# A graph network kernel: three edges of one destination per lane, packed across node tiles

## The reference

```python
# layer 0: for each type r, the mean of x[src] over a node's edges of that type, times weight[r]
out = x @ root + bias
for r in range(8):
    mask = (edge_type == r)
    sums = segment_sum(x[src] * mask[:, None], dst)
    cnt = segment_sum(mask, dst)
    out = out + (sums / maximum(cnt, 1.0)[:, None]) @ weight[r]
z = concatenate([out, x]) @ w_gate + b_gate
x = layernorm(x + tanh(out) * z + x * (1.0 - z))
# layer 1: a graph convolution with self loops and symmetric norm
h = x @ W
out = segment_sum(h[src] * (dinv[src] * dinv[dst])[:, None], dst) + b
x = layernorm(x + relu(out))
```

## Time and profile before

| | us |
|---|---|
| time, median of 3 runs | 1619.83 (1618.04 to 1620.3) |
| the profiled execution's own time | 1620.98 |
| its span in the trace | 1619.2 |
| TensorE busy | 1595.0 (99%) |
| VectorE busy | 1138.9 (70%) |
| GpSimd busy | 800.8 (49%) |
| ScalarE busy | 576.2 (36%) |

### The profile page before, as it was taken

One profiled execution on the slowest core, in us unless ns is written; L12 is line 12 of the kernel. 1 busy time (PEld: TensorE's weight loads), 2 busy tenths in 40 slices (PEclk: granted clock), 3 DMA queues, 4 the chain that ended last, 5 costly groups with the idle time before them and its releaser, 6 DMA issues.

```text
span 1619.2 us, 23695 instructions
## 1 busy us (share of the span) xinstructions
PE 1595.0 (99%) x7947; PEld 1308.0 (81%) x7947; DVE 1138.9 (70%) x1908; ACT 576.2 (36%) x963; POOL 800.8 (49%) x809
## 2 busy tenths in 40 slices
PE   8999999999999999999999999999999998999997
PEld 6888888888877777788888888888888887887886
DVE  4856655655557666748878875688778878888486
ACT  4211111111133333425655553455555653122000
POOL 1000777777766666527777772677676600000000
PEclk9999999999999999999999999999999999999999
DMA  6322444445322121267877774777778886656743
GB/s 228 109 88 79 125 125 130 113 106 138 85 77 79 66 72 64 68 221 231 250 223 222 243 234 145 227 245 222 236 217 276 296 277 208 232 211 221 281 142 117
DMA packets 122123, 280.34 MB, mean 173 GB/s; under 512 B 23142, under 2 KB 24406, under 8 KB 121872
## 3 DMA queue, kind: packets, MB, share of 16 engines
q0 software_dynamic: 38256, 104.17, 22.5%
q1 hardware_dynamic: 46912, 98.19, 18.8%
q10 hardware_dynamic: 36832, 76.44, 12.6%
HBM read 209.97 MB, written 83.10 MB: 181 GB/s over the span
## 4 chain that ended last, share of the span: by engine, by line
PE 94%; DVE 3%; DMA 1%; issue 1%; ACT 1%; POOL 0%; SPq 0%; ACTq 0%; DVEq 0%; POOLq 0%
PE PG L777 67%; PE PG L966 6%; PE PG L1032 5%; PE PM L789 3%; PE PM L800 3%; PE PM L801 3%; PE PG L873 2%; PE PG L939 2%; PE PM L835 1%; DMA y<-STAGE 1%; PE PM L948 1%; PE PM L818 1%; DMA WRAW<-in_L_gnn_weight_dram 0%; PE PM L759 0%; DVE STATS L1682 0%
## 5 line engine op out<-in xcount | busy, mean ns | idle before, releaser
L777 PE MATMUL PG<-WHI,XHI 128*128 128x512 f32 x1600 | 631.5, 395 | 2.9 <-DVE WLO L1298 2.9
L777 PE MATMUL PG<-WHI,XLO 128*128 128x512 f32 x1600 | 623.6, 390 | 0.0
L777 PE MATMUL PG<-WLO,XHI 128*128 128x512 f32 x1600 | 623.0, 389 | 0.0
L777 PEld LDWEIGHTS PG<-WHI,XHI 128*128 128x128 f32 x1600 | 300.7, 188 | 65.7 <-issue 2.9
L777 PEld LDWEIGHTS PG<-WHI,XLO 128*128 128x128 f32 x1600 | 300.6, 188 | 63.6
L777 PEld LDWEIGHTS PG<-WLO,XHI 128*128 128x128 f32 x1600 | 300.8, 188 | 60.1
L1082 ACT ACTIVATE STAGE<-PG 128x512 f32<-128x512 f32 x200 | 119.2, 596 | 460.7 <-PE PG L777 460.7
L1298 DVE TENSOR_TENSOR WLO<-WRAW,WHI 128x512 fp32r<-128x512 f32 x176 | 122.2, 696 | 226.0 <-ACT WHI L1075 225.9
L710 POOL DMA_INDIRECT WORK<-y,REC x184 | 201.6, 1096 | 93.1 <-issue 46.8
L657 POOL DMA_INDIRECT records<-RREC,IDX x160 | 210.1, 1313 | 61.0 <-issue 43.7
L710 POOL DMA_INDIRECT RAW<-y,REC x184 | 202.3, 1099 | 72.0 <-issue 46.3
(11 more groups left out here) (262 smaller groups left out, 2232.5 us busy)
## 6 DMA issues: line engine op xcount, KB each, us to landing
y<-STAGE ACTq DMA_DIRECT2D x220, 256.0 KB
WRAW<-in_L_gnn_weight_dram SPq DMA_DIRECT2D x128, 256.0 KB, 3.1
EDGE_ROWS<-edge_rows POOLq DMA_DIRECT2D x10, 1000.0 KB, 6.4
WRAW<-in_L_gnn_w_gate_dram SPq DMA_DIRECT2D x32, 256.0 KB, 4.1
WORK<-y SPq DMA_DIRECT2D x15, 512.0 KB, 4.9
WORK<-x SPq DMA_DIRECT2D x10, 512.0 KB, 4.7
WORK<-in_x_dram SPq DMA_DIRECT2D x9, 512.0 KB, 3.6
XROWS<-in_x_dram SPq DMA_DIRECT2D x9, 512.0 KB
```

What stands on the lines that cost most here:

```text
L777: last = pe.matmul(PG[:, bank, :], lhs[:, k, t * P:(t + 1) * P], rhs[:, j % 2, k, :], start=(k == 0 and n == 0), stop=(k == KT - 1 and n = ...
```

## The change

Three edges of one destination share a lane (PER = 3), and lanes are packed without a break between node tiles. A node takes a third of its edges' number, rounded up, and at least one lane, so there are 62 triples of edge tiles (NTRI) instead of 92 pairs: 186 edge tiles instead of 184.

A triple's 128 lanes can now reach from one node tile into the next. `windows` finds the node at which each triple starts (with one more matmul, `count_windows`), the number of its node tile and of the next, and two masks over the 128 rows. The one-hot puts a destination at its row modulo 128, and `msg_add` adds the bank of PM twice: to the first node tile's sums under one mask, to the next one's under the other; it loads two numbers for that.

The counts are kept with the ten source tiles of a node side by side, so one addition of 1280 cells at a computed place still does for a triple; the final stage reads them with a stride of ten elements.

Counting takes 62 steps with three tiles each (six matmuls) and two sets of one-hots in flight. In the messages VectorE adds the second and the third row, the third waiting for the second; the one-hot moves to ScalarE (Square, then Relu). The ring still has eight rows, in another order of places. Steps: run 0 in 229 to 316, run 1 in 325 to 414, the first transpose of u before step 419.

Halved scales for even source tiles (DINV_SRC) make up for counts kept doubled. The diff, cut to its core:

```diff
-NPAIR = (E // 2 + N // 2 + NT * (P - 1)) // P
-ETILES = 2 * NPAIR
+PER = 3
+NTRI = ((E + PER * N) // PER + P - 1) // P
+ETILES = PER * NTRI
...
-HIGH_CELL = 1 << 16
+HIGH_CELL = 1 << 15
+ROUND = float(3 << 22)
 SPLIT = 1024
 EXACT = 256
-AHEAD = 2
-HOTS = 8
+HOTS = 2 * PER
 EARLY = 5
 SLOTS = 4
+RAWS = 8
...
-RUN0_FROM, RUN0_TO = 229, 315
-RUN1_FROM, RUN1_TO = 324, 413
-TURN0_STEP = 417
+RUN0_FROM, RUN0_TO = 229, 317
+RUN1_FROM, RUN1_TO = 325, 415
+TURN0_STEP = 419
...
-            sp.wait_ge(msg_split, 2 * NPAIR - 2)
+            sp.wait_ge(row_added, (PER - 1) * (2 * NTRI - 1))
             load_root(0)
...
+            def row_free(row):
+
+                tri, e = divmod(row, PER)
+                if e == PER - 1:
+                    after(pool, msg_split, tri + 1)
+                else:
+                    after(pool, row_added, (PER - 1) * tri + e + 1)
...
-            def message_pair(pair, slot, run):
-
-                pair = pair + run * NPAIR
-                pe.wait_ge(pair_ready, pair + 1)
-                pe.wait_ge(msg_split, pair + 1)
-                after(pe, pair_added, pair + 1 - SLOTS)
+            def message_tri(tri, run):
+
+                slot, tri = tri % SLOTS, tri + run * NTRI
+                pe.wait_ge(tri_ready, tri + 1)
+                pe.wait_ge(msg_split, tri + 1)
+                after(pe, tri_added, tri + 1 - SLOTS)
                 pe.matmul(PM[:, slot, :], ONEHOT[:, slot, :], sp_hi[:, slot, :], start=True, stop=False)
-                pe.matmul(PM[:, slot, :], ONEHOT[:, slot, :], sp_lo[:, slot, :], start=False, stop=True).then_inc(pair_done, 1)
+                pe.matmul(PM[:, slot, :], ONEHOT[:, slot, :], sp_lo[:, slot, :], start=False, stop=True).then_inc(tri_done, 1)
...
+            def count_windows():
+                pe.wait_ge(windows_counted, 1)
+                pe.matmul(PM[:, 3, WINDOWS_AT:WINDOWS_AT + NTRI], ONES[:, :], STARTED[:, :], start=True, stop=True).then_inc(windows_summed, 1)
...
...
+            def scale_row(tri, run):
+                row = run * ETILES + PER * tri
+                act.wait_ge(got[row % RAWS], 16 * (row // RAWS + 1))
+                nc.scalar.activation(raw[row % RAWS], raw[row % RAWS], ACT.Copy,
+                                     scale=REC[:, PER * tri, 1:2].bitcast(F32)).then_inc(row_scaled, 1)
+
+            def msg_high(tri, run):
+                n, row = run * NTRI + tri, run * ETILES + PER * tri + PER - 1
+                act.wait_ge(row_added, (PER - 1) * (n + 1))
+                after(act, tri_done, n + 1 - SLOTS)
+                nc.scalar.activation(sp_hi[:, tri % SLOTS, :], raw[row % RAWS], ACT.Copy).then_inc(msg_hi, 1)
+
+            def msg_hot(tri, run):
+                n = run * NTRI + tri
+                after(act, tri_done, n + 1 - SLOTS)
+                after(act, tri_ready, n)
+                nc.scalar.activation(APART[:, :], IOTA[:, 0:P], ACT.Square, scale=-1.0,
+                                     bias=REC[:, PER * tri, 2:3].bitcast(F32)).then_inc(act_chain, 1)
+                act.wait_ge(act_chain, n + 1)
+                nc.scalar.activation(ONEHOT[:, tri % SLOTS, :], APART[:, :], ACT.Relu, scale=-1.0, bias=1.0).then_inc(tri_ready, 1)
+
+            def message(tri, run):
+                msg_hot(tri, run)
+                if tri == 0:
+                    scale_row(0, run)
+                if tri + 1 < NTRI:
+                    scale_row(tri + 1, run)
+                msg_high(tri, run)
...
+            def windows():
+
+                dve.wait_ge(windows_summed, 1)
+                link(V.tensor_scalar(BASE[:, :], PM[:, 3, WINDOWS_AT:WINDOWS_AT + NTRI], 1.0, float(NPAD - P), ALU.subtract, ALU.min))
+                link(V.tensor_copy(BASE_I[:, :], BASE[:, :]))
+                V.tensor_scalar(GROUP[:, 0, :], BASE_I[0:1, :], 7, None, ALU.logical_shift_right)
+                link(V.tensor_scalar(GROUP[:, 2, :], BASE_I[0:1, :], float(NT), None, ALU.mult))
+                link(V.tensor_scalar(BASE_I[:, :], BASE_I[:, :], P - 1, None, ALU.bitwise_and))
+                link(V.tensor_scalar(GROUP[:, 1, :], GROUP[:, 0, :], float(NT - 1), -2.0, ALU.is_equal, ALU.mult))
+                link(V.scalar_tensor_tensor(GROUP[:, 1, :], GROUP[:, 0, :], 1.0, GROUP[:, 1, :], ALU.add, ALU.add))
+                link(V.tensor_scalar(MASK[:, 1, :], BASE_I[:, :], LANE[:, 0:1], None, ALU.is_gt))
+                link(V.tensor_scalar(MASK[:, 0, :], MASK[:, 1, :], -1.0, 1.0, ALU.mult, ALU.add))
...
+            def count_add(tri):
+                at = dve.value_load(GROUP[0:1, 2, tri:tri + 1], min_val=0, max_val=(NPAD - P) * NT)
+                dve.wait_ge(cells_taken, tri + 1)
+                acc = COUNT[:, bass.ds(at, P * NT)]
+                V.tensor_tensor(acc, acc, TALLY[:, tri % 2, :].bitcast(U16), ALU.add).then_inc(cells_added, 1)
+                dve.wait_ge(cells_added, tri + 1)
+
+            def count_step(tri):
+                if tri > 0:
+                    count_add(tri - 1)
+                if tri + 1 < NTRI:
+                    count_hot(tri + 1)
+                else:
+                    count_add(tri)
...
+            def add_row(tri, e, run):
+                row, n = run * ETILES + PER * tri + e, run * NTRI + tri
+                this = raw[row % RAWS]
+                dve.wait_ge(got[row % RAWS], 16 * (row // RAWS + 1))
+                if e == 1:
+                    dve.wait_ge(row_scaled, n + 1)
+                else:
+                    dve.wait_ge(row_added, (PER - 1) * n + e - 1)
+                V.scalar_tensor_tensor(this, this, REC[:, PER * tri + e, 1:2].bitcast(F32), raw[(row - 1) % RAWS], ALU.mult,
+                                       ALU.add).then_inc(row_added, 1)
+
+            def msg_low(tri, run):
+                row, slot = run * ETILES + PER * tri + PER - 1, tri % SLOTS
+                dve.wait_ge(msg_hi, run * NTRI + tri + 1)
+                V.tensor_tensor(sp_lo[:, slot, :], raw[row % RAWS], sp_hi[:, slot, :].bitcast(F32),
                                 ALU.subtract).then_inc(msg_split, 1)
 
-            def msg_add(pair, n, run):
-                g = group_of(pair)
-                dve.wait_ge(pair_done, pair + (run * NPAIR + 1))
-                acc = U[:, bass.ds(g, 1), :].rearrange("p a n -> p (a n)")
-                V.tensor_tensor(acc, acc, PM[:, n % SLOTS, :], ALU.add).then_inc(pair_added, 1)
-                dve.wait_ge(pair_added, pair + (run * NPAIR + 1))
-
...
+            def msg_add(tri, run):
+                part = [dve.value_load(GROUP[0:1, m, tri:tri + 1], min_val=0, max_val=NT - 1) for m in range(2)]
+                dve.wait_ge(tri_done, tri + (run * NTRI + 1))
+                for m in range(2):
+                    acc = U[:, bass.ds(part[m], 1), :].rearrange("p a n -> p (a n)")
+                    last = V.scalar_tensor_tensor(acc, PM[:, tri % SLOTS, :], MASK[:, m, tri:tri + 1], acc, ALU.mult, ALU.add)
+                last.then_inc(tri_added, 1)
+                dve.wait_ge(tri_added, tri + (run * NTRI + 1))
+
+            def message_step(tri, run):
+                if run == 1 and tri == 0:
                     start_sums(1)
-                msg_sum(pair, pair % SLOTS, run)
-                if pair >= SLOTS - 1:
-                    msg_add(pair - (SLOTS - 1), pair - (SLOTS - 1), run)
-                msg_low(pair, pair % SLOTS, run)
+                add_row(tri, 1, run)
+                for e in range(2, PER):
+                    add_row(tri, e, run)
+                if tri >= SLOTS - 1:
+                    msg_add(tri - (SLOTS - 1), run)
+                msg_low(tri, run)
...
-                V.tensor_copy(counts_of(d, b)[0], CIN[b][:, :]).then_inc(c_high, 1)
+                V.tensor_copy(counts_of(d, b)[0].rearrange("p (s n) -> p s n", s=NT),
+                              CIN[b][:, :].rearrange("p (n s) -> p s n", s=NT)).then_inc(c_high, 1)
```

More of the change, by code:

```diff
@@ L82, with spread @@
 STEPS_ALL = STEPS_GEMM + 2 * NT
-def spread(start, end, count=NPAIR):
+def spread(start, end, count=NTRI):
     steps = end - start
@@ L1144, in tile_end, with steps @@
                     store_y(i, jt)
-            def steps(start, end, pairs={}, run=None):
+            def steps(start, end, tris={}, run=None):
                 for s in range(start, end):
@@ new lines, in count_setup, with count_hot @@
+                link(V.scalar_tensor_tensor(CELL[:, :], t_far, float(NT // 2), t_half, ALU.mult, ALU.add))
+            def count_hot(tri):
+                after(dve, cells_done, tri - 1)
+                for e in range(PER):
+                    tile = PER * tri + e
+                    last = V.tensor_scalar(DSTHOT[:, tile % HOTS, :], COLS[:, :], CELL[:, tile:tile + 1], WORTH[:, tile:tile + 1],
+                                           ALU.is_equal, ALU.mult)
+                last.then_inc(hot_ready, 1)
@@ L1595, in upper_gate_work, with steps @@
                     u0_low(t)
-            def steps(start, end, pairs={}, pair_step=None, messages={}, run=None):
```

(7 more changed lines are left out.)

308 lines of the change are left out of this document (134 added, 174 removed).

## The result

The changed kernel takes **1666.29 us** (median of four runs, 1661.93 to 1669.05) against 1619.28 us of the kernel before on the same chip: ratio 1.0288, 95% interval 1.0262 to 1.0314. It is slower by 47 us, where 1596 us was forecast. The profiled execution took 1669.05 us, with a span of 1667.1.

What follows compares the result with a forecast made beforehand. TensorE was taken as the bound, busy for 1595.0 of 1619.2 us. Saved matmuls, counting, window sum and tail: -27.2 + 0.55 + 0.14 + 2.5 = -24.0 us, giving a median of 1596 us, range 1590 to 1611.

Steps and rivals of the forecast that it cites:

- cover of the register loads: VectorE's message loop: two group-number loads hidden beside other work, taken as 0; up to 1.56 us per triple if uncovered.
- Rival C: VectorE's message loop exceeds its room of 3.97 us per triple; 1639 us at a loop of 4.4; chance 0.08.
- TensorE's saving: Message steps: 368 matmuls become 248, 120 fewer at 0.227 us each, so 27.2 us less.
- E: Rival: TensorE's saving isn't there because message matmuls were hidden; 1619 us; chance 0.03.
- Masked adds: VectorE's message loop: two adds to the node sums per triple, priced by a 747 ns row.
- ScalarE's one-hot: Message runs: Square and Relu of 128 columns at 0.35 us each, hidden within ScalarE's 3.0 of 4.32 us.
- D: Rival with a chance of 0.03; the prediction as given doesn't say what it claimed.
- Gathers and ring: Message runs: GpSimd's three gathers fit 4.32 us per triple, expected 3.9; the eight-row ring costs 0.
- B: Rival: the ring or the gathers hold the triples back, 1607 us at 1.47 us per gather; chance 0.16.
- The turn: Between the two message runs: the first triple is ready 2 to 3 us earlier than needed, so cost 0.
- The tail: After the messages: waits around the gate rows and first transposes of u cost +2.5 us, bounds 0 and 5.4.
- The final stage: Strided cast of the counts, at most 1.64 us against 0.79 us idle per tile, taken as 0.

Runs made afterwards that it cites:

- run 0: Not a follow-up kernel: the first of the two message runs inside the kernel, half tiles 229 to 316 in the changed kernel; no time of its own is given.
- placed loads: Changed kernel with one group-number load issued behind each of the two row additions (a run's last three behind the masked adds before); 1618.65 us, ratio 0.9988.
- windows put back: Kernel with the loads moved behind the row additions, plus the half-tile windows of before the change (229-315, 324-413, transpose 417); 1610.42 us, ratio 0.9945.

## Why the prediction was wrong, point by point

**The step that failed** is the cover of the register loads: "two loads lie beside two adds (1.44 us) and the low part before them (0.61), 2.05 us of cover against 2 x 0.78 = 1.56. I take 0". The loads stand behind the second row addition in the program, and that addition waits for the first one's result. The chain of waits in the changed kernel, from the first row addition (L1590 at 1314.45) on:

```profile
1314.45 0.68 DVE RAW L1590
...
1315.16 0.02 DVEq L1589
...
1315.22 0.32 DVE WORK L1590
...
1315.58 0.19 DVEq L1600
...
1315.86 0.30 DVEq L1600
...
1316.20 0.19 DVEq L1600
...
1316.61 0.09 DVE WORK L1604
```

L1589 is the wait for the first addition, an instruction of its own. Nothing behind it is taken up before 1315.18, so both loads have the 0.75 us of the second addition as cover and nothing else. One load is 0.30 us, its arithmetic 0.19 and its range check 0.02, with the steps between some 0.6; two are 1.2. The first masked add begins at 1316.61, 0.64 us after the second addition has ended (1315.22 + 0.75): 0.6 stay exposed. I had summed up the work that stands near the loads, and not asked from which instant the queue may fetch them. In the earlier trace rows no such wait lies between the scaled sum and the addition, which is why it showed no gap. Two smaller terms come on top: the two row additions lie 0.85 us apart, not 0.78, and even with placed loads the masked adds start 0.77 us behind the second one, not 0.66. 3.49 + 0.6 + 0.2 is the measured 4.3.

**Rival C was the right one**, named with its place (the second load) and a chance of 0.08. By its own working a loop of 4.30 us would be (4.30 - 3.97) x 124 - 10 = 31 us on top of the forecast; the two runs and the turn were 39 us above it. But a late VectorE also met the turn and the tail, which the rival left out, and the terms below came on top.

**TensorE's saving** was right in mechanism and size. With the loop under the period the stretch from half tile 229 to 399 gives 23.4 us (2.9 behind to 20.5 ahead), where 25.6 was forecast; the product was not hidden (E falls).

**Masked adds** (746 ns, x248) and **ScalarE's one-hot** were right: 397 and 311 ns against 0.35 each, and one table load, so D falls.

```profile
L1139 ACT ACTIVATE APART<-IOTA,REC 128x128 f16<-128x128 f16 x124 | 49.3, 397 | 11.1 <-ACT STAGE L1107 6.4 <-ACT STAGE L1166 3.5 <-PE PM L821 0.9
L1142 ACT ACTIVATE ONEHOT<-APART 128x128 fp32r<-128x128 f16 x124 | 38.5, 311 | 3.9
```

**Gathers and ring.** The gathers were to fall to 0.99 us with the one-hot gone from VectorE. They did not: with the placed loads the groups of run 0 have 1117 and 1128 ns (the earlier trace rows had 1114), with issue 1.42 us, three in 4.26 of 4.32 (in the changed kernel, whose loop is slower, 1060 and 1065 from 740 to 992 us). The reading from the earlier trace rows rested on two gathers, yet the rest of that trace bears it out: from 726 to 992 us the 74 gathers that overlap a one-hot average 1.23 us, the 42 beside a scaled sum alone 1.01 and the other 59 1.03. What it missed is that the row additions, now two to a triple, take the one-hot's place: with the placed loads the 116 gathers beside a row addition average 1.18 us, the other 62 1.01. Why a sum alone didn't lengthen them before isn't tested. The sum stood, since both values fitted, and B falls. The prediction had drawn on the Trainium skill (SBUF — State Buffer, Who interferes with whom), where GpSimd and a VectorE operation in a two-port mode block each other. The trace before agrees as far as it goes (1.23 us beside a one-hot, 1.02 for all others); no run here shows in which mode the one-hot ran.

**The turn.** Taken at 0, it cost 8.6 us. The sums of run 0 were stored at 1027.28 us (1001.55 before), the bias was asked for at 1038.72, and two of the last three additions stood 1.40 and 1.62 us with both loads bare. With the placed loads it costs 1.0 us: the ten half tiles were enough.

**The tail** was taken at +2.5 (bound 5.4). From half tile 399 to the last product of the hidden stage the placed loads lose 16.4 us of their lead, and the windows put back save 11 of that at this point (7 by the ratios of the medians). The mechanism was there, the term mis-sized. In the timeline of VectorE with the placed loads the gate sums stand ahead of a weight split and of the upper rows' XLO, and later VectorE waits for the high part of u:

```profile
1307.47 1.22 DVE L1754 TENSOR_TENSOR GATE<-GATE,X 128x1024 f32<-128x1024 f32 x1
1308.72 1.22 DVE L1755 TENSOR_TENSOR GATE<-GATE,BIAS_GATE 128x1024 f32<-128x1024 f32 x1
1309.98 0.69 DVE L1334 TENSOR_TENSOR WLO<-WRAW,WHI 128x512 fp32r<-128x512 f32 x1
1310.59 0.68 DVE L1637 TENSOR_TENSOR XLO<-PG,XHI 128x512 fp32r<-128x512 f32 x1
...
1318.33 0.69 DVE L1732 TENSOR_TENSOR SPLO<-PM,SPHI 128x512 fp32r<-128x512 f32 x1 [6.46 <-ACT SPHI L1226]
```

TensorE waited 3.1 us for that XLO, and its windows show what came with it (columns: stretch, length, busy, granted clock, DMA share, GB/s):

```profile
1290.00:1310.00 20.00, 17.30 (x77) 1.00 0.62 211
1310.00:1330.00 20.00, 15.21 (x56) 0.83 0.85 305
```

Over these 40 us it is idle for 7.5 us, where it was idle for none before and 1 to 3 was the sign of being right. I had priced the wait for the split at 0.9 us, and the clock at nothing. In the changed kernel VectorE's backlog came on top.

**The final stage** was taken at 0 after looking at the cast alone. Its bound of 1.64 us held (1426 ns); the subtraction, which reads the same counts with the same stride, I had left out. Together 0.6 + 1.1 = 1.7 us per node tile against 0.79 of slack: 5.5 us.

**Start of the counting**, taken at 0: 0.5 to 3.3 us at half tile 160 in the traces of the kernels that start it at 150, and 7.6 in the profiled execution after. The sorted records were there 6.8 us later than before (VectorE took them up at 459.72, before at 452.96). What held the sort's scatters up I haven't tested.

Together: the placing of the loads is 47 us, which is the whole of the slowdown. That the rest is about 0 and not the forecast's -24 is, in the traces, the tail and hidden stage (15.5 more than forecast), the final stage (5.5), the runs (2.2) and the counting (2.2). These four terms come from one execution of the placed loads, which was 3.6 us above its median, so they are too large by about that in all.

## What to carry to other kernels

Before a load or register operation is called hidden, find the last wait ahead of it on its engine: only work that runs after that wait is released can cover it. Here one load behind each operation longer than itself was hidden, while two in a row left something bare in each loop that had them (0.6, 0.71 and, on average, 0.14 us). A loop's gap costs nothing as long as the loop's sum stays under the period of the engine that sets the pace, so sum the loop with its gaps, and then price every reader of a changed layout, not just the first.

## What the runs showed of the hardware

**Register loads.** In the changed kernel a load with its arithmetic and range check takes some 0.6 us of VectorE's queue with the steps between, and two follow each other; in other kernels of these experiments up to a third of them take longer, one 1.2 us (source view of the changed kernel: duration min/median/max in ns, first and last start):

```profile
L1600 DVEq TENSOR_LOAD <-GROUP x248: 296/303/668, 743.5 to 1353.7; - x124
L1600 DVEq FUSED_REGOPS  x248: 190/190/190, 744.2 to 1354.1; - x124
L1600 DVEq SEQ_ASSERT  x248: 23/23/23, 744.5 to 1354.3; - x124
```

**A stride of ten 16-bit elements** makes VectorE's operations on the counts 1.74 times as long (cast 820 to 1426 ns, subtraction 1492 to 2592), and ScalarE's same strided cast takes 2654 ns. The Trainium skill (SBUF — State Buffer, Door 1: The DMA port swizzle) lets 16-bit elements be strided for free up to 8, by lines of 16 bytes; ten elements are 20 bytes, and the rows agree that this stride isn't free. No other stride was run, so where it begins to cost isn't shown.

**A wait costs TensorE more than its length.** At the start of the counting in the changed kernel it stood idle for 3.74 us and then ran at the lower clock (columns: stretch, length, TensorE busy, granted clock, DMA share, GB/s; 1.00 is 2.4 GHz, 0.50 is 1.2):

```profile
456.00:460.00 4.00, 4.00 (x19) 1.00 0.67 208
460.00:464.00 4.00, 0.45 (x2) 0.84 0.05 18
464.00:468.00 4.00, 3.81 (x12) 0.50 0.00 0
468.00:472.00 4.00, 4.00 (x18) 0.81 0.46 137
```

Over these 40 us (440 to 480) TensorE issued 159 matmuls where the kernel before issued 190, and came out 7.4 us behind from a wait of half that length.
